# First sum pass of a graph kernel: two pairs of count banks in place of three, and a second bank for block products

## The reference

```python
def sage_conv(x, edge_index, W_l, b_l, W_r, num_segments):
    agg = segment_sum(x[src], dst, num_segments)
    return agg @ W_l.T + b_l + x @ W_r.T
h = relu(sage_conv(x, ...))                      # layer 0, first sum: over x
x = layernorm(x + sage_conv(h, ...))             # layer 0, second sum
en, ev = (x @ W2s + b2s)[src], (x @ W2d + b2d)[dst]          # layer 1, attention
alpha = softmax over the edges of a target of sum(leaky_relu(en + ev) * attn)
msg = softmax(en * edge_attr * alpha)            # over the 32 features
x = layernorm(x + (x + segment_sum(msg, dst).sum(heads)) @ W1 + b1)
```

## Time and profile before

| what | us |
|---|---|
| median of three runs | 4071.0 (4070.92 to 4072.41) |
| the profiled execution, its own time | 4068.59 |
| its span, first to last instruction | 4066.6 |
| stretch of the first sum pass in it | 68 to 1060 |
| in that stretch of 992.0: PE busy | 905.43 |
| ACT busy | 810.44 |
| DVE busy | 687.26 |
| POOL busy | 673.17 |

### The profile page before, as it was taken

The page is one execution under the profiler, slowest core; times in us unless marked ns, Lnnn a source line. Parts: engine busy times, 40 slices in busy tenths (PEclk is TensorE's granted clock), DMA queues, the critical chain, the costliest instruction groups (busy, mean ns, idle before and its releaser), DMA issues. The chain is left out here.

```text
span 4066.6 us, 79597 instructions
## 1 busy us (share of the span) xinstructions
PE 3054.0 (75%) x26497; PEld 2336.8 (57%) x26497; DVE 2564.1 (63%) x7531; ACT 2697.1 (66%) x7419; POOL 2903.5 (71%) x2913
## 2 busy tenths in 40 slices
PE   4899999999798998885566666766766667666655
PEld 2555555666466666665465555665656666556544
DVE  7987766555422222235357777778777787777776
ACT  4888888778665556641056767777668766677745
POOL 4677777776377777755777777777777777777735
PEclk9999999999899999997657777777667776677767
DMA  2455565555588888853333333333333433343311
GB/s 79 186 207 207 211 234 208 206 207 206 195 310 279 291 289 284 284 173 107 64 86 85 83 81 87 89 86 84 79 82 93 91 83 83 77 92 87 87 31 41
DMA packets 294489, 592.92 MB, mean 146 GB/s; under 512 B 121210, under 2 KB 205364, under 8 KB 286169
## 3 DMA queue, kind: packets, MB, share of 16 engines
q1 hardware_dynamic: 203920, 515.15, 36.0%
q0 software_dynamic: 88192, 72.56, 11.0%
q10 hardware_dynamic: 1969, 0.10, 0.0%
HBM read 384.60 MB, written 202.94 MB: 144 GB/s over the span
## 5 line engine op out<-in xcount | busy, mean ns | idle before, releaser
L897 ACT ACTIVATE scratch<-sum_x_ps_c 128x600 bf16<-128x600 f32 (+7 forms) x1003 | 775.4, 826 | 168.1 <-PE sum_x_ps_c L934 156.5
L1945 POOL DMA_INDIRECT scratch<-fs_scratch,src_idx x728 | 725.3, 996 | 221.9 <-issue 221.9
L834 POOL DMA_INDIRECT gath<-in_x,src_idx x620 | 673.2, 1086 | 277.4 <-issue 182.4
L834 POOL DMA_INDIRECT gath<-y_scratch,src_idx x540 | 524.2, 971 | 171.6 <-issue 163.4
L2073 ACT ACTIVATE scratch<-scratch,bias,weight 128x32 f32<-128x32 f32 x1360 | 484.0, 399 | 101.5 <-DVE bias L2143 101.5
L1987 PEld LDWEIGHTS ps_e<-fdw,scratch 128*128 128x128 f32 x3136 | 500.4, 242 | 24.2
L934 PE MATMUL sum_x_ps_c<-e_tab,scratch 128*128 128x300 bf16 (+7 forms) x2006 | 472.9, 323 | 51.9 <-DVE scratch L1012 32.3
L1009 DVE TENSOR_SCALAR e_tab<-scratch 128x1300 bf16<-128x1300 f16 (+13 forms) x1024 | 455.7, 458 | 61.0 <-PE sum_x_ps_c L934 53.0
L1987 PE MATMUL ps_e<-fdw,scratch 128*128 128x66 f32 x3136 | 482.7, 322 | 0.0
L2154 DVE SCALAR_TENSOR_TENSOR scratch<-ps_e,attn_sb 128x128 f32<-128x128 f32 x784 | 190.2, 285 | 424.3 <-PE ps_e L1987 423.3
L963 PEld LDWEIGHTS sum_x_ps_d<-parts,scratch 128*128 128x128 bf16 x5800 | 337.1, 98 | 158.7 <-ACT scratch L897 68.0
(11 more groups left out here) (341 smaller groups left out, 6362.9 us busy)
## 6 DMA issues: line engine op xcount, KB each, us to landing
count_scratch<-scratch SPq DMA_DIRECT2D x58, 3200.0 KB
scratch<-count_scratch SPq DMA_DIRECT2D x232, 800.0 KB
onehot<-rel_scratch SPq DMA_DIRECT2D x196, 256.0 KB
scratch<-in_edge_attr_2x SPq DMA_DIRECT2D x390, 128.0 KB
fdw<-fd_scratch SPq DMA_DIRECT2D x392, 33.0 KB
scratch<-fs_scratch,src_idx POOLq DMA_INDIRECT x728
gath<-in_x,src_idx POOLq DMA_INDIRECT x652
gath<-y_scratch,src_idx POOLq DMA_INDIRECT x540
```

Of the source, the lines that this page charges most:

```text
L834: pool.indirect_dma_start(out=gath[:, s, t, 0:F], out_offset=None, in_=table_dram, in_offset=bass.IndirectOffsetOnAxis(ap=src_idx[:, g, k: ...
L897: act.activation(to, ps_c[u % pairs][:, :, 0:q].rearrange("p h (d a) -> p h a d", d=d), ACT.Copy).then_inc(kept, 1)
L1945: pool.indirect_dma_start(out=rows_of(m)[:, t, :], out_offset=None, in_=fs_dram, in_offset=bass.IndirectOffsetOnAxis(ap=src_idx[:, g, k:k ...
```

## The change

It makes the pass over x use the layout that the second pass has: two pairs of banks for counts rather than three, and block products that go in turn to `ps_d` and to the first bank of the pair that is freed, `ps_c[2]`. A count of unit u now waits for the keep of unit u − 2 instead of u − 3. The product of block j waits until the sums of block j − 2 are read, instead of block j − 1.

```diff
-            lent, pairs = (slots, 2) if read else (0, 3)
+            lent, pairs = slots if read else 0, 2
...
                 def product_of(j):
-                    return ps_c[2][:, 0, 0:3 * F] if read and j % 2 else ps_d[:, 0:3 * F]
+                    return ps_c[2][:, 0, 0:3 * F] if j % 2 else ps_d[:, 0:3 * F]
...
                             if i == 0:
...
-                                if read and j >= 2:
+                                if j >= 2:
                                     pe.wait_ge(summed_up, j - 1)
-                                elif not read and j:
-                                    pe.wait_ge(summed_up, j)
```

## The result

The changed kernel took 4089.7 us in the median of five runs (4084.3 to 4094.3), the kernel before 4070.9 in five runs on the same chip (4069.9 to 4072.4): ratio 1.0041, 95% interval 1.0029 to 1.0052. Run again beside another set of runs, the ratio was 1.0026 (1.0017 to 1.0035). So it is slower by some 7 to 21 us; 4081 had been forecast, with 4067 to 4100 as the range.

A forecast was written before the change was run, and what follows sets the result against it. The first sum pass was taken as bound by the hand-over between PE and ACT, no engine full. Holds +12.9 and product bank −2.7 gave +10.2 us on 4071.0, thus 4081, with 8 in 10 for 4067 to 4100.

The forecast's parts named there:

- That the end of a block costs nothing: Block ends, first pass: counts held one keep earlier cost nothing, covered by PE's existing wait for the last keep.
- The holds inside blocks, +12.9 us: Inside first-pass blocks: longest hold of each of 27 runs ending with idle ACT, 11.5 us, plus 1.4 us for restarts.
- The second product bank, −2.7 us: First-pass block starts: PE's wait for DVE's reduction goes in six starts, winning 2.7 us, between 0 and 6.3.
- The sum: First pass and program: 12.9 − 2.7 = +10.2 us, giving 4081 us.
- holds add up: Rival, first pass: each of 27 runs pays one more hold; +24 us, range 4089 to 4110; chance 0.16.
- The clock: First sum pass, 992.0 us long, was read as running at the full granted clock, 1.00.
- PE's waits came as written: Sign: PE's keep waits in counts grow from 9.4 to 40–70 us, fall at product starts; reduction wait gone.
- ACT's wait for counts was to rise by 10 us: Sign, first pass: ACT's wait rises about 10 us from 156.5, mostly within 10 us behind the feature copies.
- A wait that stays at 156 us: Sign against the forecast: ACT's wait staying at 156 us despite the holds would mean the queue covers them.
- the queue covers more: Rival, first pass: slack makes held runs cost half or nothing, 0 to 6.4 us; 4068 to 4075; chance 0.26.
- The product banks decide: Rival, block starts: all 14.6 us of DVE's reductions leave the path; 4054 to 4067 us; chance 0.08.

The follow-up runs named there:

- the wait alone: Kernel before with its three pairs and one product bank; only the first pass's count wait names the keep two units back; ratio 1.0036.
- The first edit alone: Kernel before with two pairs of count banks, all block products still in one bank; ratio 1.0039.
- the kernel with the delay: Kernel before, first pass unchanged; behind it ACT copies a finished table onto itself six times; 4096.1 us, ratio 1.0044.
- quarters, three: Kernel before (three pairs), each of ACT's 25 feature copies cut into four of 128 columns in four successive steps; ratio 1.0041.
- quarters, two: The whole change (two pairs), each of ACT's feature copies cut into four of 128 columns in four successive steps; ratio 1.0073.

## Why the prediction was right, and where not

*That the end of a block costs nothing:* right, within 1 us. With the wait alone, the last keep of each block and the three behind it lose 0.7 us in sum (places behind a copy and at a fall of the clock left out). PE's waiting moved from 40.7 us at products, of which 11.4 are left, to the last counts.

*The holds inside blocks, +12.9 us:* right in mechanism, too small. The first edit alone cost 17.2 us, some 18.5 without the clock's falls. Read keep by keep, 14.3 us arose within the first twelve keeps behind a feature copy (up to the end of its block), 214 of 1003 units, in the first pair of profiles, in the second, and with the wait alone. The forecast had 10.1 us there, for 13 copies; the traces show a loss of 0.2 us or more behind 20 of the 25. Counting one hold for each run of keeps was nearer than counting all: PE's waits for keeps in counts rose by 37 us, and 14 were lost. What it left out is that a keep that isn't ready also loses its overlap with the one before; that this makes up the difference is not shown.

*The second product bank, −2.7 us:* right. Of the 2.8 us between the last keeps with one bank and with two, 1.5 are the clock. But at the six starts where the reduction had been late (units 107, 358, 386, 670, 842 and 968) the changed kernel gains 0.6, 0.3, 0.5, 0.6, 0.5 and 0.6 us on the kernel before, 3.0 in all, and the estimate against one bank is some 2. The Trainium skill's rule that banks rotate (Perfetto Trace Analysis, Optimizing Tensor Performance, Matmuls) holds in direction. The trace had shown its size: six late reductions out of 57.

*The sum:* +10.2 us forecast for pass and program; the pass took +14.4 in both pairs of profiles (some 16 without the clock's falls), the program +17 and +11 by its two ratios. The term that was mis-sized is the one for holds, 12.9 against 17.2. The first median, 4089.7, lies above the 4076 to 4088 that the forecast was given, in the range of "holds add up"; that the second set lands on the forecast's +10 is luck, since the pass had lost more.

*The clock:* the prediction read the pass as being "at the full granted clock, 1.00". That is its mean, rounded; the two stretches at 0.50 in it are worth 3 us, more than the term for the product bank.

*Signs in the profile:* PE's waits came as written. One sign was wrong: ACT's wait for counts was to rise by 10 us and fell by 1.4; the loss stands in ACT's busy time and its lost overlap. A wait that stays at 156 us was to mean that the queue covers the holds. It stayed, and they were not covered.

*The rivals:* "the queue covers more" is refuted by the pass's 14 us, though with copies on DVE it is most of what happens. "Holds add up" put the holds at 26.4 us; with 17.2 measured, and some 18.5 without the clock's falls, they lie between it and the forecast. "The product banks decide" is refuted by the kernel with one product bank.

*What stays open:* why the change costs more with the copies at block starts (17.9 us) than inside (14.4); without the clock's falls it is some 20 against 16. That ACT's copies make most of it was shown by taking them off ACT; that the length of a single copy matters was not borne out.

## What to carry to other kernels

A spare buffer between two engines that are near balance is worth what interrupts the consumer: look in the trace for work of another kind between its instructions, read how far the producer runs ahead there, and count one hold for each run that ends dry. The better cure may be where the producer's own side work stands: PE's turns, moved to where PE waited for ACT anyway, brought 26 to 28 us, where the third pair is worth 17. Busy time may rise when an engine is fed late, since its instructions then no longer overlap. And before a few microseconds are read from a pass, the places where the granted clock fell in each trace have to be set against one another.

## What the runs showed that I had not expected

The part behind the pass, the same instructions in each of these kernels, took from 3002 to 3018 us in single profiles. Stretches by window, in the kernel before, its second profile, and the kernel with the delay:

```profile
1060.00:4066.00 3006.00, 2120.05 (x16930) 1752.37 (x16930) 1829.61 (x5283) 1864.71 (x6373) 2180.39 (x2218) 0.77 0.46 128
```

```profile
1059.00:4061.00 3002.00, 2121.68 (x16930) 1752.22 (x16930) 1826.77 (x5283) 1864.48 (x6373) 2175.37 (x2218) 0.76 0.45 128
```

```profile
1081.00:4099.00 3018.00, 2118.31 (x16930) 1749.42 (x16930) 1827.16 (x5283) 1865.58 (x6373) 2186.09 (x2218) 0.77 0.45 127
```

The mean granted clock, the column behind POOL's, doesn't order them: 0.76 stands at the shortest, 0.77 at the other two. In totals, the kernel before ran from 4065.0 to 4081.0 us over the sets of runs, and took 4063.3 in its second profile. Its first three runs, within 1.5 us, had suggested a finer measure than there is.

A change of a few microseconds in one pass is told by that pass's own end in the trace. It came back within 1 us for the two kernels that were profiled twice, but 5.5 us later in the kernel with the delay, whose pass is unchanged. What moves it is the clock, which falls at other places in each execution. All stretches at 0.50 in the first pass, by their start, and an estimate of the pass without them (0.4 us for those near 120 us, 1.5 for each other one of 3.4 us, 2.7 for each that is twice as long, from the prices read above):

| kernel | first keep to last, us | clock at 0.50 from, us | without, us |
|---|---|---|---|
| before | 981.2 | 142, 890 | 978 |
| before, second profile | 980.1 | 120, 260 | 978 |
| delay behind the pass | 986.4 | 120, 141 (long), 196, 264, 892 (long) | 978 |
| changed | 994.6 | nowhere | 995 |
| changed, second profile | 994.5 | nowhere | 995 |
| wait alone | 998.2 | 657 | 997 |
| one product bank | 998.4 | 657 | 997 |
| copies on DVE, three pairs | 975.7 | 121, 141, 752 | 972 |
| copies on DVE, two | 976.8 | nowhere | 977 |
| copies at block starts, three | 952.3 | 121, 142 | 950 |
| copies at block starts, two | 970.2 | nowhere | 970 |
| quarters, three | 1001.1 | 142, 262, 498, 712 (long), 771, 941 | 991 |
| quarters, two | 1013.7 | 260, 537, 718 (long), 830 | 1007 |
| turns at block ends, copies inside | 954.4 | 120 | 954 |

In each pair, the kernel with two pairs of banks has fewer such stretches. What makes the clock fall in one execution and not in the next, at the same place and behind the same work, stays open.
